# The opening and first four units of an attention + Hadamard-FFN kernel, written out call by call, with split first transfers, zero-tile matmuls and three rotations on VectorE

## What is computed

```python
x = x + attn(layernorm(x), wq, wk, wv, wo)      # 16 query heads, 4 key/value heads, head size 128
#   q, k: rotary embedding; scores * exp(-lam_h * (i - j)) for i >= j, else 0; then times v; then wo
x = x + ffn(layernorm(x), W1, W2, W3)           # fwht(silu(x W1.T) * (x W3.T)) W2.T, hidden size 1024
```

## Time and profile before

| | |
|---|---|
| median of 3 runs (lowest, highest) | 277.31 us (277.09, 278.17) |
| the profiled execution | 277.34 us, its span 275.5 us |
| busy share: TensorE, VectorE, ScalarE, GpSimd | 93%, 75%, 61%, 56% |
| instructions: matmuls, VectorE, ScalarE, GpSimd | 1480, 324, 279, 111 |
| TensorE's waits in all, of which before its first matmul | 14.6 us, 7.7 us |
| chain that ended last: TensorE, VectorE, GpSimd | 70%, 13%, 5% |

### The profile page before, as it was taken

How to read it: one execution, slowest core, us unless ns; L and a number is a source line. 1 busy time by engine, 2 the same in 40 slices (tenths; PEclk the granted TensorE clock), 3 DMA queues, 4 the chain that set the end, 5 groups by cost and what they waited for, 6 DMA issues and landing times.

```text
span 275.5 us, 4150 instructions
## 1 busy us (share of the span) xinstructions
PE 257.6 (93%) x1480; PEld 225.1 (82%) x1480; DVE 206.1 (75%) x324; ACT 167.1 (61%) x279; POOL 153.2 (56%) x111
## 2 busy tenths in 40 slices
PE   0796878999999999999999999999999999999995
PEld 0584766898898988878888888898989879988895
DVE  2878799899997988967999898795756985144433
ACT  2586787678689767655667777995352552043230
POOL 1049989978878935813597787899709400000000
PEclk9999999999999999999999999999999999999999
DMA  7695022102022000000002002200000000200002
GB/s 259 242 355 190 0 80 77 59 20 76 4 76 76 0 2 0 1 4 0 0 2 76 2 0 76 76 4 1 2 0 0 2 0 0 79 0 0 2 0 76
DMA packets 5203, 13.23 MB, mean 48 GB/s; under 512 B 576, under 2 KB 2112, under 8 KB 5184
## 3 DMA queue, kind: packets, MB, share of 16 engines
q1 hardware_dynamic: 4752, 12.65, 13.0%
q10 hardware_dynamic: 432, 0.33, 0.4%
HBM read 11.93 MB, written 1.05 MB: 47 GB/s over the span
## 4 chain that ended last, share of the span: by engine, by line
PE 70%; DVE 13%; POOL 5%; issue 5%; ACT 3%; DMA 3%; SPq 0%; DVEq 0%; POOLq 0%
PE bank L274 24%; PE bank L275 23%; PE bank L276 23%; DVE rope_b L780 3%; POOL qk L647 2%; POOL q_hid L654 2%; DVE rope_a L779 2%; DMA w_raw<-in_wq 1%; DMA x_sb<-in_x 1%; PE bank L287 1%; DVE xn L748 1%; DVE rope_b L817 1%; DVE w_lo L754 1%; POOL w_lo L659 1%; DVE p_lo L798 1%
## 5 line engine op out<-in xcount | busy, mean ns | idle before, releaser
L647 POOL TENSOR_TENSOR qk<-rope_a,rope_b 128x512 f32<-128x512 f32 x40 | 53.5, 1341 | 34.8 <-DVE rope_b L780 34.4
L274 PE MATMUL bank<-xt_hi,w_hi 128*128 128x512 f32 x144 | 57.4, 398 | 1.5 <-DVE rope_a L779 0.8
L275 PE MATMUL bank<-xt_lo,w_hi 128*128 128x512 f32 x144 | 56.9, 395 | 0.0
L276 PE MATMUL bank<-xt_hi,w_lo 128*128 128x512 f32 x144 | 56.6, 393 | 0.0
L654 POOL TENSOR_TENSOR q_hid<-qk,q_hid 128x512 fp32r<-128x512 f32 x32 | 43.0, 1355 | 9.7 <-ACT q_hid L515 9.7
L780 DVE TENSOR_TENSOR rope_b<-rope_b,sin_sb 128x512 f32<-128x512 f32 x40 | 42.1, 1053 | 0.0
L522 ACT ACTIVATE p_hi<-bank 128x512 fp32r<-128x512 f32 x48 | 28.6, 596 | 15.7 <-DVE bank L793 15.2
L779 DVE TENSOR_TENSOR rope_a<-bank,cos_sb 128x512 f32<-128x512 f32 x40 | 27.5, 686 | 14.2 <-ACT rope_b L510 13.5
L275 PE MATMUL bank<-w_lo,o_hi 128*128 128x256 f32 x128 | 36.2, 283 | 0.0
L276 PE MATMUL bank<-w_hi,o_lo 128*128 128x256 f32 x128 | 36.2, 283 | 0.0
L274 PE MATMUL bank<-w_hi,o_hi 128*128 128x256 f32 x128 | 36.1, 282 | 0.0
(11 more groups left out here) (72 smaller groups left out, 591.4 us busy)
## 6 DMA issues: line engine op xcount, KB each, us to landing
w_raw<-in_w SPq DMA_DIRECT2D x6, 512.0 KB, 3.3
w_raw<-in_wq SPq DMA_DIRECT2D x4, 512.0 KB, 4.8
decay_sb<-in_decay SPq DMA_DIRECT2D x4, 512.0 KB, 6.3
w_raw<-in_wo SPq DMA_DIRECT2D x4, 512.0 KB, 3.2
x_sb<-in_x SPq DMA_DIRECT2D x4, 256.0 KB, 4.5
out<-x_sb SPq DMA_DIRECT2D x8, 128.0 KB, 1.8
w_raw<-in_wk SPq DMA_DIRECT2D x1, 512.0 KB, 4.7
w_raw<-in_wv SPq DMA_DIRECT2D x1, 512.0 KB, 6.6
```

Source lines behind the costliest of these rows:

```text
L274: pe.matmul(o, a_hi, b_hi, start=first, stop=False, skip_group_check=shared)
L275: pe.matmul(o, a_hi, b_lo, start=False, stop=False, skip_group_check=shared)
L276: return pe.matmul(o, a_lo, b_hi, start=False, stop=last, skip_group_check=shared)
L647: pool.tensor_tensor(qk[:, r % 2, :], rope_a[:, r % 2, :], rope_b[:, r % 2, :], ALU.add).then_inc(rope_sum, 1)
```

## The change

- The chunks wv and wk change places (0 and 2). Of wk the first 256 columns (head K0) and of wq the first 512 (heads Q0, Q1) are loaded, copied and subtracted first, as pieces of their own (`FIRST`, `load_first`, `high_first`, VectorE's `low_first`); the rest of the chunk follows.
- The second sequence of x goes out on ScalarE's queue, ahead of the identity; cos and sin move from there to SP, behind the first pieces and chunks 0 and 1.
- The first normalisation: tiles 0 and 1 on VectorE, 2 and 3 on ScalarE (with a shift).
- GpSimd clears half of o_hi, and TensorE runs 16 matmuls of 512 columns on it into bank 7 before the first transposition, 2 more before K0; their results are not used.
- K0's projection issues its four products with xt_hi before the two with xt_lo.
- For the rotations K0, Q0, Q1 sum and low part are made by VectorE (`rope_add`, `low_rope` of its own, with semaphores of their own).
- Low parts of chunks 0, 3, 5, 7 are VectorE's, all others GpSimd's.
- From the opening to the end of unit 3, each engine has a list of calls instead of the loop, in another order; the loops begin at unit 4 (`FIRST_UNIT`) with the same bodies. Up to there both programs issue the same set of products.

```diff
@@ -55,7 +55,7 @@
 AT_W2 = AT_K
 AT_FF = AT_Q
-CHUNKS = [("wk", 0, AT_K), ("wq", 0, AT_Q), ("wv", 0, AT_V), ("wq", 1, AT_Q + CH), ("wo", 0, AT_O),
+CHUNKS = [("wv", 0, AT_V), ("wq", 0, AT_Q), ("wk", 0, AT_K), ("wq", 1, AT_Q + CH), ("wo", 0, AT_O),
           ("wq", 2, AT_Q + 2 * CH), ("wo", 1, AT_O + CH), ("wq", 3, AT_Q + 3 * CH), ("wo", 2, AT_O + 2 * CH),
           ("wo", 3, AT_O + 3 * CH),
           ("w1", 0, AT_FF), ("w3", 0, AT_FF + CH), ("w1", 1, AT_FF + 2 * CH), ("w3", 1, AT_FF + 3 * CH),
@@ -63,12 +63,18 @@
 CHUNK_NO = {(w, i): n for n, (w, i, _) in enumerate(CHUNKS)}
 SLOTS = 3
 FIRST_CHUNKS = 5
-LOW_ON_DVE = 4
-START = ([("X", 0, k) for k in range(KD)] + [("K", 0, 0), ("Q", 0, 0), ("V", 0, 0), ("Q", 0, 1), ("V", 0, 1),
-          ("Q", 0, 2), ("V", 0, 2), ("Q", 0, 3), ("V", 0, 3)])
+FIRST = ((2, 0, D), (1, 0, 2 * D))
+FIRST_OF = {n: at for n, _, at in FIRST}
+WARM_FIRST, WARM_NEXT = 16, 2
+LOW_ON_DVE = (0, 3, 5, 7)
+START = [("X", 0, k) for k in range(KD)] + [("K", 0, 0), ("Q", 0, 0), ("Q", 0, 1), ("V", 0, 0), ("V", 0, 1), ("V", 0, 2), ("V", 0, 3), ("Q", 0, 2), ("Q", 0, 3)]
...
             load_x(0)
-            for n in range(3):
-                load_chunk(n)
+            load_first(0)
+            load_first(1)
+            load_chunk(0)
+            load_chunk(1)
+            sp.dma_start(cos_sb[:], cos).then_inc(tables_loaded, 16)
+            sp.dma_start(sin_sb[:], sin).then_inc(tables_loaded, 16)
+            load_chunk(2)
             load_chunk(3)
             load_decay(0)
             load_chunk(4)
             load_decay(1)
-            load_x(1)
+            load_x(2)
+            load_x(3)
...
+            def warm(times):
+                for _ in range(times):
+                    pe.matmul(bank[7][:], o_hi[:, 0, 0, 0:P], o_hi[:, 0, :, :], start=True, stop=True)
...
-                wait_low_weights(pe, CHUNK_NO[chunk])
+                if h < 2 - (kind == "K"):
+                    pe.wait_ge(first_lo, 1 + (kind == "Q"))
+                else:
+                    wait_low_weights(pe, CHUNK_NO[chunk])
                 at = (AT_K if kind == "K" else AT_Q) + h * KD * P
+                if item == ("K", 0, 0):
+                    for k in range(KD):
+                        pe.wait_ge(x_hi_done, k + 1)
+                        a = slice(at + k * P, at + (k + 1) * P)
+                        pe.matmul(o[:], w_hi[:, a], xt_hi[:, k, :], start=k == 0, stop=False)
+                        pe.matmul(o[:], w_lo[:, a], xt_hi[:, k, :], start=False, stop=False)
+                    for k in range(KD):
+                        pe.wait_ge(lin_free, LIN_NO[("X", c, k)] + 1)
+                        a = slice(at + k * P, at + (k + 1) * P)
+                        last = pe.matmul(o[:], w_hi[:, a], xt_lo[:, k, :], start=False, stop=k == KD - 1)
+                    last.then_inc(lin_full, 1)
+                    return
                 for k in range(KD):
                     pe.wait_ge(lin_free, LIN_NO[("X", c, k)] + 1)
                     a = slice(at + k * P, at + (k + 1) * P)
...
-            pe.wait_ge(tables_loaded, 48)
-            fill(START)
-            for u in range(UNITS + 1):
+            pe.wait_ge(zeroed, 1)
+            warm(WARM_FIRST)
+            pe.wait_ge(ident_loaded, 16)
+            turn(0, 0)
+            turn(0, 1)
+            warm(WARM_NEXT)
+            project(("K", 0, 0))
+            project(("Q", 0, 0))
+            project(("Q", 0, 1))
+            project_values(0, 0)
+            project_values(0, 1)
+            project_values(0, 2)
+            project_values(0, 3)
+            project(("Q", 0, 2))
+            scores(0, S_FIRST0)
+            scores(0, S_SECOND)
+            project(("Q", 0, 3))
+            scores(0, S_FIRST1)
+            project(("Q", 0, 4))
+            project(("Q", 0, 5))
+            attend(0, 0)
+            scores(1, S_FIRST0)
+            scores(1, S_SECOND)
+            scores(1, S_FIRST1)
+            project(("K", 0, 1))
+            project(("Q", 0, 6))
+            attend(0, 1)
+            project(("Q", 0, 7))
+            project_out(0, 0)
+            attend(1, 0)
+            project_out(0, 1)
+            scores(2, S_FIRST0)
+            scores(2, S_SECOND)
+            scores(2, S_FIRST1)
+            attend(1, 1)
+            project(("Q", 0, 8))
+            project(("Q", 0, 9))
+            project_out(1, 0)
+            attend(2, 0)
+            project_out(1, 1)
+            scores(3, S_FIRST0)
+            project(("K", 0, 2))
+            scores(3, S_SECOND)
+            attend(2, 1)
+            scores(3, S_FIRST1)
+            project(("Q", 0, 10))
+            project(("Q", 0, 11))
+            project_out(2, 0)
+            attend(3, 0)
+            for u in range(FIRST_UNIT, UNITS + 1):
                 if u < UNITS:
                     scores(u, S_FIRST0)
                     scores(u, S_SECOND)
...
-            act.dma_start(ident_sb[:], ident).then_inc(tables_loaded, 16)
-            act.dma_start(cos_sb[:], cos).then_inc(tables_loaded, 16)
-            act.dma_start(sin_sb[:], sin).then_inc(tables_loaded, 16)
-            high_weights(0)
+            act.dma_start(x_sb[:, 2:4, :], x[1]).then_inc(x_loaded[1], 16)
+            act.dma_start(ident_sb[:], ident).then_inc(ident_loaded, 16)
+            high_first(0)
+            high_first(1)
+            norm_apply(0, range(2, 4))
             high_x(0, 0)
             high_x(0, 1)
+            high_weights(0)
             high_weights(1)
-            high_weights(2)
-            high_weights(3)
             swap(("K", 0, 0))
             swap(("Q", 0, 0))
-            high_v(0, 0)
             high_rope(("K", 0, 0))
             swap(("Q", 0, 1))
+            high_v(0, 0)
             high_v(0, 1)
+            high_v(0, 2)
             high_rope(("Q", 0, 0))
+            high_rope(("Q", 0, 1))
+            high_weights(2)
+            high_v(0, 3)
             swap(("Q", 0, 2))
-            high_v(0, 2)
-            high_rope(("Q", 0, 1))
+            high_weights(3)
             swap(("Q", 0, 3))
-            high_v(0, 3)
+            high_p(0, S_FIRST0)
             high_rope(("Q", 0, 2))
-            high_p(0, S_FIRST0)
+            swap(("Q", 0, 4))
+            high_p(0, S_SECOND)
             high_rope(("Q", 0, 3))
-            high_p(0, S_SECOND)
+            swap(("Q", 0, 5))
+            high_p(0, S_FIRST1)
             high_weights(4)
-            for u in range(UNITS):
...
+            high_p(3, S_FIRST0)
+            swap(("K", 0, 2))
+            high_o(2, 1)
+            high_p(3, S_SECOND)
+            high_rope(("Q", 0, 9))
+            swap(("Q", 0, 10))
+            high_rope(("K", 0, 2))
+            swap(("Q", 0, 11))
+            high_p(3, S_FIRST1)
+            high_o(3, 0)
+            for u in range(FIRST_UNIT, UNITS):
...
             pool.memset(minus_half[:], -0.5).then_inc(half_set, 1)
+            pool.memset(o_hi[:, 0, :, :].bitcast(F32), 0.0).then_inc(zeroed, 1)
             pool.wait_ge(half_set, 1)
             inverse_deviation(0)
-            rope_add(("K", 0, 0))
-            rope_add(("Q", 0, 0))
-            low_rope(("K", 0, 0))
-            rope_add(("Q", 0, 1))
-            low_rope(("Q", 0, 0))
-            low_rope(("Q", 0, 1))
+            low_weights(1)
+            pool.wait_ge(rope_lo_dve, DVE_ROPES)
+            low_weights(2)
             rope_add(("Q", 0, 2))
             rope_add(("Q", 0, 3))
             low_rope(("Q", 0, 2))
             low_rope(("Q", 0, 3))
+            rope_add(("Q", 0, 4))
             low_weights(4)
-            for u in range(UNITS):
+            low_rope(("Q", 0, 4))
+            rope_add(("Q", 0, 5))
+            rope_add(("K", 0, 1))
+            low_rope(("Q", 0, 5))
+            low_rope(("K", 0, 1))
+            rope_add(("Q", 0, 6))
+            low_weights(6)
+            rope_add(("Q", 0, 7))
+            low_rope(("Q", 0, 6))
+            low_rope(("Q", 0, 7))
+            rope_add(("Q", 0, 8))
+            rope_add(("Q", 0, 9))
+            low_rope(("Q", 0, 8))
+            rope_add(("K", 0, 2))
+            low_rope(("Q", 0, 9))
+            low_rope(("K", 0, 2))
+            inverse_deviation(1)
+            rope_add(("Q", 0, 10))
+            rope_add(("Q", 0, 11))
+            low_weights(8)
+            for u in range(FIRST_UNIT, UNITS):
...
-            for t in range(TT):
-                tile_stats(0, t)
-            norm_variance(0)
-            norm_apply(0, range(TT))
-            low_weights(0)
+            tile_stats(0, 0)
+            tile_stats(0, 1)
+            tile_stats(0, 2)
+            tile_stats(0, 3)
+            tile_mean(0, 0)
+            tile_mean(0, 1)
+            tile_mean(0, 2)
+            tile_mean(0, 3)
+            add_eps(0)
+            norm_shift(0)
+            norm_apply(0, range(0, 2))
+            low_first(0)
+            low_first(1)
             low_x(0, 0)
             low_x(0, 1)
-            low_weights(1)
-            low_weights(2)
```

(106 more changed lines are left out.)

128 lines of the change are left out of this document (94 added, 34 removed).

## The result

The changed kernel takes 272.48 us (272.0 to 272.83, four runs) beside 277.2 for the kernel before on the same chip, a ratio of 0.9824 (95% interval 0.9807 to 0.9841). The forecast was 272.8. Its profiled execution took 272.2 us against 277.34 before.

What follows compares the result with a forecast made beforehand. VectorE and TensorE were both near their limits before attend(3, 1), with VectorE setting the pace. First scores at 21.3 + 45.7 work + 0.6 idle = 67.6 against 72.06, so 277.34 - 4.5 = 272.8 us; range 269.6 to 275.6.

Steps and rivals of the forecast that it cites:

- One instant decides: At attend(3, 1), 72.06 us before: whatever is saved ahead of it moves the end equally; forecast 4.5 us earlier.
- The opening: Up to the first scores: they come at about 21.3 us instead of 27.51, with VectorE setting this time.
- The delay of 0.2 charged for the zero tiles: Before the first transposition: the sixteen zero-tile matmuls were taken to delay the opening by 0.2 us.
- Rival 5: First key projection: zero tiles do not lift the clock before K; at most 1.0 us later, 273.8; no chance given.
- VectorE's list: First scores to attend(3, 1): VectorE's passes sum to 45.7 us, plus 0.6 idle, giving attend(3, 1) at 67.6.
- TensorE alone: TensorE up to attend(3, 1): 42.0 us of work after 21.3 gives 63.3, 8.8 us earlier, but it waits for VectorE.
- rival 1: Up to attend(3, 1): TensorE sets the end as VectorE's waits shrink; gain up to 8.8 us, 268.5; chance 0.12.
- Rival 2: Loading x: both halves land together at 4.70, so rstd is 0.7 us later, 273.5; chance 0.10 as decisive difference.
- Lie in the wait for the transpositions: Opening: VectorE's two weight pieces, about a quarter and a half of 1.21 us, fall within that wait.
- Rival 3: Hand-written orders make VectorE, ScalarE and GpSimd wait in turn; 3.5 us idle instead of 0.6, 275.7; chance 0.13.
- Rival 4: Rotations: VectorE meets GpSimd at its worst each time, weight parts slow too; 6.4 us, 279.2; chance 0.08.
- Costing chunks 5 and 7 at 2.4 us on the limiting engine: Before attend(3, 1): moving their low parts gives GpSimd 2 x 2.41 us back and costs VectorE 2.4.

Runs made afterwards that it cites:

- stats_late: Changed kernel with the second token half's statistics, mean and epsilon moved to unit 4, shift and normalisation to unit 5; 273.62 us, ratio 0.9876.
- the second profile: Profile of the changed kernel run again, unaltered, as yardstick for another set; 272.9 us, ratio 0.9852.
- v_more: Changed kernel plus ten unused statistics passes on VectorE in units 0 to 3; 274.55 us, ratio 0.9915.
- eps_late: Changed kernel with only the last tile's statistics, mean, epsilon and the second half's shift moved behind unit 3; 272.41 us, ratio 0.9810.
- low57_pool: Changed kernel with the low parts of chunks 5 and 7 back on GpSimd; 273.74 us, ratio 0.9882.
- ropes_pool: Changed kernel with sums and low parts of rotations K0, Q0, Q1 back on GpSimd; 274.93 us, ratio 0.9895.
- units_only: Changed kernel keeping the unit lists, with most of the opening put back (unsplit weights, no zero tiles, x on SP, rotations on GpSimd); 276.09 us, ratio 0.9945.

## Why the prediction was right, and where it wasn't

**One instant decides: right.** The gain at attend(3, 1) is 72.06 - 66.87 = 5.19 us, the profiled executions differ by 277.34 - 272.2 = 5.14. In thirteen of the fourteen profiles the span behind that instant is 203.4 to 203.7 us. The exception is stats_late, which moves work across it: the reason given ("the state of the other engines is the same in both programs") is the condition, and that kernel breaks it.

**The opening: right.** rstd ends at 6.03 + 1.02 = 7.05 (said 7.1). GpSimd's half of wq starts at 11.41, a microsecond before it was expected, and its first rotation at 23.97 (said: none until 22). First scores 20.96 or 21.25 for 21.3; with 20.96 to 21.73 in eight profiles of the same opening, the nearness is partly luck. The sum left out what spreads them, ScalarE's copy of wq's piece ahead of its two tiles.

**Which parts make the opening.** Here the sum named none as decisive. Counted from ScalarE's first normalised tile, the first scores are 2.3 later without the split, 2.0 with the rotations on GpSimd, 0.6 without the zero tiles. GpSimd, in order of time:

```profile
0.76 0.52 POOL L842 MEMSET o_hi<- 128x512 f32 x1
...
11.41 1.82 POOL L820 TENSOR_TENSOR w_lo<-w_raw,w_hi 128x512 fp32r<-128x512 f32 x1 [4.37 <-ACT w_hi L599]
```

The memset took 0.52, inside its bounds of 0.1 to 1.3, and half a chunk 1.82 instead of 1.2. The delay of 0.2 charged for the zero tiles did not show: their last ends as the transpositions begin at 7.71, and without them these began at 7.80, once VectorE had normalised the first tile. In the second profile they ended at 7.99 and may have held up the first transposition, but there the fourth waited for ScalarE's tile until 8.70 in any case. Rival 5, that they don't lift the clock before the first key projection, was wrong, since its starts are 0.23 to 0.30 apart. Their worth, 0.6, lies inside the forecast's 0 to 1.0. Most of the old loss of 9 x 0.19 is gone without them too: three slow starts, and the pace near 0.23 from 11.18 on.

**VectorE's list: right in sum, by errors that cancel.** Forecast were 45.7 of work and 0.6 of idle time, 46.3 in all; measured were 45.91 between the instants, 0.45 of them idle. The wait of each second product was 1.018 - 0.67 = 0.35, not 0.49: 12 x 0.14 = 1.7 us less. The list left out one pass, the low output of (3, 0), which the changed kernel has between the low score tile (65.45) and attend(3, 1), 0.6 more: 34 passes. Three weight parts at 1.21 were right. The other 0.9 is spread: the epsilon took 0.74 for a tile of four columns (0.17 in the opening), and 34 passes at 0.61 make 0.3. The 0.35 is no constant either: with the same twelve rotations the mean second product was 0.90 us in v_more, 0.97 in stats_late, 1.10 in eps_late and 1.14 in low57_pool. Work moved to or from VectorE moves these waits too, and that the sum came out is luck in part. TensorE's last wait is for that low output, not for the low score. The busy claim, over 97% from 21 to 67, came out at 45.75 of 46.20, or 99%.

**"TensorE alone ... 63.3. It could be 8.8 us earlier but waits for VectorE": this step was wrong in its size.** If it were so, 2.5 us less on VectorE would have moved the instant by about 2.5. It moved the distance by 0.6, and there VectorE idled while TensorE was full. More work on VectorE, 3.3 to 3.7, moved it by 2.2 with VectorE busy throughout, so in the changed kernel VectorE does set the pace, but only just. TensorE was busy 43.35 between the instants, not 42.0. And 1.34 of its waiting, at attend(0, 0), hardly answers to VectorE's load: it stands at 1.31 to 1.34 in all eleven profiles with the unit lists. Most of these add or take work only elsewhere. Two are a test: from the first scores to the end of this wait VectorE is busy 7.26 us of 8.06 in ropes_pool and 6.66 of 8.07 in units_only, where it is 8.47 of 8.51 in the changed kernel, and the wait stays 1.34 and 1.33. But VectorE's last passes before it run without a break in ropes_pool too (27.14 to 30.81), and none of them was taken out. I read the wait from the order as a chain, since mask, exact part and low part of a score tile follow one another on two engines with three projections beside them; another order was not tried, so that it belongs to the order is not shown. The 0.41 at attend(1, 0) goes when chunk 5's low part leaves VectorE (low57_pool has no wait there) and stays when the statistics leave: where the pass stands counts, not the sum. With both, TensorE's own limit for this order is 43.35 + 1.34 + 0.41 = 45.1, about what stats_late reached (45.31). The spare was 0.8 us, and rival 1 (268.5) asked for what isn't there. Of the five waits foretold, those at attend(1, 0), at attend(3, 0) and before attend(3, 1) came; those at attend(0, 1) and scores(2, 0) did not, and the largest, at attend(0, 0), was not named.

**Rival 2, x landing together: it happened, and was priced at the wrong place.** The halves, issued at the same time, landed 3.2 and 3.4 us later, and the four statistics passes run without a break from 3.99. The sum took them as in the old trace, 3.71 and 4.70; the rival's 4.70 was pessimistic too, and rstd stayed at 7.05. The trace thus bears out the Trainium skill's page "DMA: Bandwidth & Descriptors", section "Issuing engines are not separate DMA queues". The 0.7 that I hung on the statistics was not lost against the old kernel; against one queue 0.24 is (the shift at 7.08, not 6.84). "Lie in the wait for the transpositions" held for VectorE's two weight pieces and not always for ScalarE's copies of them: its tiles begin as soon as the shift is there in the changed kernel's first profile, 0.3 later in its second, 0.8 later in the two kernels with loops.

**Rival 3, handovers: wrong for the lists, right for the loops.** The lists left 0.45 us of idle time on VectorE. With the loops the new opening yields 275.5 to 276.2, close to the rival's 275.7.

**Rival 4, the port: wrong.** The longest second products took 1.4 (64.11), but the mean fell from 1.16 to 1.02, and the weight parts stayed at 1.21. Both costs exist: in low57_pool the mean was 1.14, in v_more one weight part took 1.93.

**Costing chunks 5 and 7 at 2.4 us on the limiting engine** told half the story. Put back they cost 0.8 us in time and 1.6 between the instants, for want of rotated heads at 54.79 and by 1.5 us more in VectorE's second products.

The 6.5 us won by the first scores are thus kept but for 1.4. VectorE does 45.46 - 41.06 = 4.4 us more between the instants, and idles 3.05 less.
